# Six-layer network: the softmax normalisation moves from VectorE to the pool engine (GpSimd), between its powers and its cosine products

## The reference, cut to what matters

```python
qkv = shift_tokens(x) @ Wqkv                       # 16 heads of 64
q, k = l2norm(q) * q_scale, l2norm(k) * k_scale    # per head
q = q * cos * scale + rotate_half(q) * sin * scale # rotary, k with 1/scale
sim = q @ k.T * 8                                  # window: 64 queries, 96 keys
attn = softmax(sim)                                # the step that the change moves
x = attn @ v @ Wo + x
x = x + W2(a * gelu(gate)), (a, gate) = split(layernorm(shift_tokens(x)) @ W1)
```

## Time and profile before

| | us |
|---|---|
| median of 3 runs | 5706.67 (5686.42 to 5718.4) |
| the profiled execution, its own time | 5696.51 |
| its span | 5694.7 |
| PE, DVE, ACT, POOL busy | 4468.9, 3603.6, 2963.1, 1958.8 |

### The profile page before, as it was taken

How to read it: one execution, slowest core, us unless ns; L and a number is a source line. 1 busy time by engine, 2 the same in 40 slices (tenths; PEclk the granted TensorE clock), 3 DMA queues, 4 the chain that set the end, 5 groups by cost and what they waited for, 6 DMA issues and landing times. The chain is left out here.

```text
span 5694.7 us, 89214 instructions
## 1 busy us (share of the span) xinstructions
PE 4468.9 (78%) x28284; PEld 3096.7 (54%) x28284; DVE 3603.6 (63%) x7261; ACT 2963.1 (52%) x8154; POOL 1958.8 (34%) x1203
## 2 busy tenths in 40 slices
PE   6887987888644458888888888888888888588788
PEld 4655665555411136666666666666666666355566
DVE  5554224455578867777777777777777777344422
ACT  3333434443233336666666666666666666233433
POOL 3433003232045444444444444444444434122300
PEclk8888999999755579999999999999999999566799
DMA  0000000000000010000000000000000000000000
GB/s 18 1 2 35 0 0 20 1 1 14 3 0 0 0 50 1 0 0 22 0 0 22 0 0 22 0 0 22 0 0 0 0 0 1 17 1 0 0 30 7
DMA packets 26280, 41.43 MB, mean 7 GB/s; under 512 B 12112, under 2 KB 18664, under 8 KB 25448
## 3 DMA queue, kind: packets, MB, share of 16 engines
q1 hardware_dynamic: 26088, 39.04, 2.0%
HBM read 36.93 MB, written 2.10 MB: 7 GB/s over the span
## 5 line engine op out<-in xcount | busy, mean ns | idle before, releaser
L1426 PE MATMUL ps<-l2f_wqkv,l2f_xsT 128*128 (+3 forms) x1536 | 741.4, 605 | 97.1 <-DVE xnT L1621 90.3
L1358 POOL TENSOR_TENSOR l2f_rn<-l2f_ss,neghalf 128x16 f32<-128x16 f32 x192 | 564.7, 2941 | 436.1 <-DVE l2f_ss L1615 436.1
L1803 ACT ACTIVATE l2f_p<-ps,l2f_negmax 128x96 f32<-128x96 f32 x1536 | 501.7, 338 | 282.7 <-DVE l2f_negmax L1646 279.1
L1364 POOL TENSOR_TENSOR l2f_cosd<-xnT,l2f_rot 128x1024 f32<-128x1024 f32 x192 | 487.2, 2542 | 174.8 <-DVE xnT L1621 174.8
L1484 PE MATMUL ps<-l2f_pT,l2f_vw 96*128 96x128 f32 x3072 | 423.1, 281 | 40.4 <-DVE l2f_pT L1668 40.4
L1426 PEld LDWEIGHTS ps<-l2f_wqkv,l2f_xsT 128*128 128x128 f32 (+1 forms) x1536 | 243.4, 178 | 347.8 <-issue 197.4
L1818 ACT COPY l2f_oT<-ps 64x256 f32<-64x256 f32 x768 | 281.3, 366 | 269.8 <-PE ps L1484 258.3
L1484 PEld LDWEIGHTS ps<-l2f_pT,l2f_vw 96*128 96x128 f32 x3072 | 381.7, 195 | 61.4 <-issue 56.5
L1384 POOL TENSOR_TENSOR l2f_rstd<-l2f_mv,neghalf 128x1 f32<-128x1 f32 x96 | 52.8, 550 | 1051.5 <-DVE l2f_mv L1680 1051.5
L1457 PEld LDWEIGHTS ps<-l2f_kT,l2f_qz 128*128 128x128 f32 x3072 | 399.2, 194 | 1.4 <-issue 0.3
L1457 PE MATMUL ps<-l2f_kT,l2f_qz 128*128 128x96 f32 x3072 | 398.7, 273 | 0.0
(11 more groups left out here) (354 smaller groups left out, 10607.0 us busy)
## 6 DMA issues: line engine op xcount, KB each, us to landing
l2f_wqkv<-L_ffn_Wqkv_dram SPq DMA_DIRECT2D x18, 512.0 KB
l0f_w<-L_w_dram SPq DMA_DIRECT2D x2, 2304.0 KB
l3f_w<-L_w_dram SPq DMA_DIRECT2D x2, 2048.0 KB
l2f_wo<-L_ffn_Wo_dram SPq DMA_DIRECT2D x6, 512.0 KB
l2f_w<-L_ffn_W_dram SPq DMA_DIRECT2D x6, 341.0 KB
l2f_b<-L_ffn_b_dram SPq DMA_DIRECT2D x6, 341.0 KB
l1f_w<-L_w_dram SPq DMA_DIRECT2D x1, 1152.0 KB
k_turn<-l3a_kF SPq DMA_DIRECT2D x4, 256.0 KB, 2.0
```

Source lines behind the costliest of these rows:

```text
L1358: nc.gpsimd.tensor_tensor(rn[:, k], ss[:, k], g.neghalf[:, 0:HEADS], ALU.pow).then_inc(rn_ready, 1)
L1364: nc.gpsimd.tensor_tensor(cosd[:, k].rearrange("p (h d) -> p h d", d=DH), nrm[:, k].rearrange("p (h d) -> p h d", d=DH), rot[:, k, 0, t].u ...
L1426: ins = nc.tensor.matmul(g.ps[0:rows, 2 * (k % 2) + hf], x, wqkv[:, bass.ds(weight_slot(it), 1), c0 + hf * 512:c0 + (hf + 1) * 512] .rearr ...
L1803: ins = nc.scalar.activation(p[:, n % 2, c], g.ps[:, 4, c * KW:(c + 1) * KW], ACT.Exp, bias=negmax[:, col:col + 1], accum_out=rowsum[:, co ...
```

## The change

Three edits, all in `l2_ffn_stage`. DVE's `scale` becomes `inverse_sums`: the reciprocal alone. The product `p * rinv` goes to POOL's program as a new `scale`, called at four places in its slot. In that slot `scaled_rotary` also moves, from between the two `inverse_norms` to behind the second. And ACT's `copy_q` makes two copies of 64 partitions by 1024 columns instead of four of 512.

```diff
@@ POOL
+            def scale(it, t, i):
+                if t is None:
+                    return
+                n = PER * t + i
+                pool.wait_ge(rinv_ready, at(it, STEPS2, n + 1))
+                nc.gpsimd.tensor_tensor(
+                    p[:, n % 2], p[:, n % 2],
+                    rinv[:, QUAD * n:QUAD * (n + 1)].unsqueeze(2).broadcast_to([P, QUAD, KW]), ALU.mult).then_inc(scaled, 1)
+
             def slot(ahead, now, behind):
                 inverse_deviation(*behind)
+                scale(*now, 0)
                 inverse_norms(*ahead, 0)
+                scale(*now, 1)
+                inverse_norms(*ahead, 1)
                 scaled_rotary(*ahead)
-                inverse_norms(*ahead, 1)
                 cosines(*ahead, 0)
+                scale(*now, 2)
                 cosines(*ahead, 1)
+                scale(*now, 3)
@@ DVE
-            def scale(it, t, i):
+            def inverse_sums(it, t, i):
                 if t is None:
                     return
                 n = PER * t + i
                 dve.wait_ge(probs_ready, at(it, STEPS2, n + 1))
                 nc.vector.reciprocal(rinv[:, QUAD * n:QUAD * (n + 1)],
                                      rowsum[:, QUAD * n:QUAD * (n + 1)]).then_inc(rinv_ready, 1)
-                dve.wait_ge(rinv_ready, at(it, STEPS2, n + 1))
-                nc.vector.tensor_tensor(
-                    p[:, n % 2], p[:, n % 2],
-                    rinv[:, QUAD * n:QUAD * (n + 1)].unsqueeze(2).broadcast_to([P, QUAD, KW]), ALU.mult).then_inc(scaled, 1)
@@ DVE slot
-                scale(*now, 0)
+                inverse_sums(*now, 0)
...
-                scale(*now, 1)
+                inverse_sums(*now, 1)
...
-                scale(*now, 2)
+                inverse_sums(*now, 2)
...
-                scale(*now, 3)
+                inverse_sums(*now, 3)
@@ ACT copy_q
                     for hf in range(2):
                         rows = slice(hf * DH, (hf + 1) * DH)
-                        for c in range(0, PAIRS, 4):
-                            ins = nc.scalar.copy(qz[rows, c:c + 4, t % 2, :, hf],
-                                                 g.ps[rows, c // 4].rearrange("p (c j q) -> p c j q", c=4, q=QB))
-                        ins.then_inc(q_copied, 1)
+                        nc.scalar.copy(qz[rows, :, t % 2, :, hf],
+                                       banks(0, 2)[rows].rearrange("p (c j q) -> p c j q", j=QBS, q=QB)).then_inc(q_copied, 1)
```

## The result

The changed kernel takes **6082.3 us** (6045.5 to 6119.7) where the kernel before, on the same chip, takes 5705.0: a ratio of 1.0664, 95% interval 1.0584 to 1.0745, 377 us slower. The forecast was 6005, in a range of 5885 to 6200.

What follows compares the result with a forecast made beforehand. No engine is full; the slot is a chain walking from engine to engine. 73 slots at 2.57 us and 23 at 4.8 add 298 to 5696.5, giving 5995; with 10.2 for the median, 6005 us, range 5885 to 6200.

Steps and rivals of the forecast that it cites:

- Step 1: POOL's second product waits behind the power of the q norms; turn 1 and maxima 3 come 2.56 us late.
- Step 2: Swap 0 no longer waits for POOL's cosines, saving 1.19 us; normalize 1 is 1.37 late, the third product hidden.
- Step 3: POOL's last product waits behind the second cosines and rotate 0; turn 3 is 3.9 us late, mix 2.57 a slot.
- Two wide copies: ACT's copy_q as two copies of 1024 columns takes 2.02 us instead of 2.15; at most 12 us in all.
- Table slots: In 23 slots POOL's rotary tables, behind the second power, delay cosines and normalize 1; each slot grows 4.8 us, 110 together.
- The order: POOL's queue order in the stage costs 2.57 us in 73 slots and 4.8 in 23, 298 us in all.
- its fall: Rival, 10%: TensorE's granted clock falls from 1.00 to 0.81 in the stage, 270 us more, 6275 us.
- VectorE's time decides: Rival, 4%: in each slot the chain loses DVE's product time and swap 0's wait; 307 us faster, 5400 us.
- POOL takes the port first: Rival, 17%: POOL's last product goes straight on after the second cosines and rotate 0 waits; 214 us more, 5921 us.
- DVE keeps the port: Rival, 13%: gate_hidden and swap 1 go ahead of POOL's waiting last product; 459 us more, 6166 us.
- GpSimd's price: POOL's product takes 0.825 us where DVE's takes 0.56, 1.5 times as long, not about 2 times.

Runs made afterwards that it cites:

- Experiment 2: Two runs on the changed kernel: POOL's product of step 1 ahead of the first power, 6021.6 us; that of step 3 ahead of the second cosines, 6014.5 us.
- the filled kernel: The changed kernel with 9 dummy 128x128 matmuls on PE ahead of turn 1 and again ahead of turn 3: 6040.8 us, ratio 1.0583.
- experiment 3: The changed kernel with POOL's second product ahead of the first power, third ahead of the first cosines, fourth ahead of the second cosines: 5894.5 us, ratio 1.0317.

## Why the prediction was right

Shifts below are of the slot at full clock, both kernels counted from the slot's first reciprocal (before 2832.01, after 3044.06).

- **Step 1** held: the second product starts with the end of the power, turn 1 comes 2.51 late (forecast 2.56), maxima 3 likewise 2.51. Experiment 2 adds what the step alone would not tell: removing this wait gives back 61 us, not 2.5 a slot, because the next late product takes its place.
- **Step 2** held: swap 0's stall is gone, normalize 1 is 1.32 late (1.37), the product of step 2 is hidden.
- **Step 3** held: the product comes behind rotate 0, turn 3 is 3.79 late (3.87), gate_hidden waits for it. Mix comes 2.39 late (2.57): copy_q follows copy_hidden at once, 0.16 sooner than reckoned. Two wide copies take 2.04 (2.02).
- **Table slots**: 33.9 were forecast. The eight at a clock of 1.00 take 33.30, 4.24 more than the 29.06 of before where 4.8 had been reckoned; the slots about the median, 34.4, and above it are at 0.90. Normalize 1 starts 2.2 us later there than in a plain slot (16.34 after the first reciprocal, at 2596.10, against 14.13), where the forecast put 2.9: the product of step 2, which was to slip in while swap 0 waited, came behind all of swap 0 by its times (1.27 us from 2595.59, where swap 0 ends at 2596.18).
- **The order was put too high, by some 30 us.** At a clock of 1.00 (for tile 0, which has no such slot, in the filled kernel) the slots give 48 x 2.39 + 23 x 2.32 + 23 x 4.24 = 265 us; the forecast had 298.
- **The term left out of the sum is the clock.** The forecast took PE's clock as 1.00 and kept its fall as a rival of 10%, priced at 0.81 with 270 us. It fell to 0.92, below the 0.95 that the prediction itself had named as a sign that it was wrong. Of the 374 us that the stage lost in the profiled executions, the 110 beyond the order are slots at the lower clock; priced as the rival was, with half of PE's longer time on the path, 0.92 gives an estimate of 24.0 x (1/0.92 - 1) / 2 x 96 = 100. How much of the median's 377 is clock is less sure: some 110 if the median execution is like the traced one in the stage alone, some 60 if it also has the 49 us that the traced one lost outside the stage.
- **In part it is luck.** An order put too high and a clock put at nothing partly cancel, and the forecast ends up 77 us short. The range held the result because its upper end had been drawn for a rival, DVE keeping the port, that did not come true in the changed kernel.
- **The rivals.** *VectorE's time decides*: excluded, taking the products away altogether gives 51 us. *POOL takes the port first*: not here, the last product took 1.81, 0.98 longer than alone, and came behind rotate 0. *DVE keeps the port*: not in the changed kernel, where the product came ahead of gate_hidden, but it happens in another order (experiment 3). The Trainium skill's rule on the shared ports (SBUF — State Buffer, "Who interferes with whom") gives the order of the changed kernel; with experiment 3 it does not agree by the trace's starts, where the cosines start at 2503.52, rotate 0 at 2503.58, and the cosines wait.
- GpSimd's price: 0.83 and 0.56, as the earlier trace rows had it, not the factor of 2 that the Trainium skill advises with (GPSIMD Engine Reference, "When to use GPSIMD").

## What to carry to other kernels

An engine that is idle 60% of a slot is not idle when you need it: before work is moved to it, put its queue in order of time and see what each new instruction stands behind, and what then stands behind it. Ask first what removing the work altogether would give: here 51 us, so the move had little to win. And a wait put on TensorE is paid a second time where it takes the granted clock down, even if the other steps of the slot are reckoned to a few tenths of a microsecond. Read each slot with its own clock before you put its length down to the order of the work.

## What the runs showed of the hardware that was not expected

- The clock is sensitive to where PE stands still. The kernel before waits up to 1.7 us and holds 1.00 in every plain slot but one, though nine of its 23 table slots are at 0.94 or less; with two waits of 2.3 us in a plain slot it is 0.92 in the stage, with those two filled 0.99 again. It differs from slot to slot in one execution: plain slots of 30.72 and of 33.49 us are the same instructions, and a wait of 3.45 us stands in table slots of the filled kernel at 1.00 and at 0.91 alike. What decides between them was not tried.
- The same unchanged work behind the stage ran at a granted clock of 0.74 in the trace of the kernel before and of 0.65 in that of the changed one, 41 us longer. A second kernel, with the tables early, shows 0.65 and the same 41 us; the filled one shows 0.74 and none. Why is not known.
- A POOL instruction can be passed by several DVE instructions: the second cosines of experiment 3 took 5.12 us instead of 2.35 while rotate 0, gate_hidden and both halves of swap 1 went through, while in the changed kernel a POOL product got in between rotate 0 and gate_hidden. No run tells why the two differ.
